# LSTM products moved behind the GRU's gates, routing to step 1, and a third bank for the expert products, in a one-core kernel of two recurrences, attention and a mixture of experts

## The chip, the cores and the metric

One core of one Trainium2 chip. The metric is the device time of one execution in microseconds (us). Median, lowest and highest of the runs are given below. All times in the text are us unless they say ns.

## The reference, cut to what matters

A block over a batch of 16 sequences of 128 steps, width 128:

```python
h   = LSTM(x, h0)                       # 128 steps, one after the other
x1  = x + causal_attention(h)           # 16 heads of 64, low-rank keys and values (32)
g   = GRU(x1, h0)                       # 128 steps; after every 4th: h = tanh(h @ Wp + bp)
out = x1 + sum over the top 2 of 8 experts of w_e * (gelu(g @ w1_e + b1_e) @ w2_e + b2_e)

# one step of the GRU
z, r = sigmoid([x_t, h] @ Wz + bz), sigmoid([x_t, h] @ Wr + br)
h_cand = tanh([x_t, r * h] @ Wh + bh)
h = (1 - z) * h + z * h_cand
```

Causality lets everything run as one pipeline: attention for a block of 8 steps needs only LSTM states up to it, the GRU needs only `x1` up to its step, the experts need whole blocks of 128 tokens (8 steps by 16 sequences).

## The kernel before, in words

The program is one loop over k, written out by hand for each engine: `for k in range(STEPS)` stands in the TensorE (PE), ScalarE (ACT), VectorE (DVE), GpSimd (POOL) and SyncE (SP) blocks. At k the LSTM does its step t = k and the GRU its step g = k - 18. Everything else is put into the loop at fixed residues of k modulo 8. I call these *step 0* to *step 7*. Each engine works its queue strictly in order, so that the order in the source is the schedule, and semaphores (`wait_ge`, `then_inc`) tie the queues together.

TensorE, per k: `g_step` (the GRU's gate products), then `turn_probs` (transposes of the attention's probabilities, steps 4 to 7, bank `pC`), `values` (steps 5, 6, 7, 0, bank `pV`), `project` (step 1), `lat_q` (step 0: latents into `pY`, queries into `pC`), an `experts_down` of slot A (bank `pV`, steps 2, 3, 4), then `g_candidate`, `l_step` (the LSTM's 12 recurrent products), `expert_up` half 0, `g_fill` (step 1), `experts_down` of slot B (bank `pY`, steps 2 to 6), `g_propagate`, `l_fill` (step 7: the LSTM's input products of the next eight steps, 9 products), `expert_up` half 1, `route_x` (step 2) and `scores` (steps 2 to 5). `expert_up` stands in steps 6, 7, 0 and 1.

The GRU's chain through the engines in one k: `g_step` (PE), `gT` = tanh (ACT), `gRZ` (DVE), `g_candidate` (PE), `gC` = tanh (ACT), `gB`, `ghi`, `g`, `glo` (DVE), next `g_step`. The LSTM's: `l_step`, `lT` (ACT), `lP`, `oK`, `lT[4]` (DVE), `lC` (ACT), `hhi`, `hfull`, `hlo` (DVE). A value is kept as a sum of two f16 parts (hi and lo), hence the three products for each matrix.

Waits that matter below:

- `expert_up` of half h waits until ScalarE has read the half before it out of the bank (`gelu`); on ScalarE that read (`activate`, tile `hid`) of half 1 stands behind `gC` and behind `pt_copy` (tile `PThi`).
- `lat_q` writes the latents into columns 384 to 511 of `pY`; `lat_copy` (DVE, tile `latT`) reads them. An expert product that goes into `pY` in this step waits for it: `pe.wait_ge(lat_done, count(latents_at, k + 1))`.
- `q_rest` (DVE, tile `qh`) ends the queries; SP then spreads them with four transfers for each group of four sequences (`spread_queries`, tile `qbd`), and `scores` waits for these.
- `TO_EXP` and `TO_GELU` name the k at which ScalarE changes its function table, with an activation into `spare`.

## Time and profile before

| | us |
|---|---|
| median of 3 runs | 589.99 |
| lowest, highest | 588.25, 590.3 |
| the profiled execution | 591.56 |
| its span in the profile | 589.7 |
| TensorE busy | 525.5 (89%) |
| VectorE busy | 424.1 (72%) |
| ScalarE busy | 352.9 (60%) |

The engines' shares are averages over three stages: LSTM and attention alone (k below 18, to about 63 us), the filling pipeline (k = 18 to 49, to about 190 us), and the full pipeline after that (to about 491 us), followed by a tail without the LSTM. The full pipeline repeats every eight k, so that one such period stands for all. Its time starts at the first product of `g_step` of step 0.

### The profile page before, as it was taken

Reading aid. Unit: us, or ns where it says so; the run is one execution under the profiler, and the core shown is the slowest. Engines: PE = TensorE matmul, PEld = TensorE weight load, DVE = VectorE, ACT = ScalarE, POOL = GpSimd, SP = SyncE. Lnnn points to the kernel's source line nnn. Section 1 sums busy time; section 2 is a strip of 40 time slices with the busy share of each in tenths; the row PEclk is TensorE's granted clock in tenths of the full one; section 3 lists DMA queues with packets and bytes.
Section 4 is the critical chain, followed back from the end, with each engine's and each line's share of the span. In section 5 each row is a group of like instructions: output and inputs, shape, how many; then the busy total and the mean of one; then the engine's idle time right before and its main releaser. Section 6 shows DMA issues by size and latency. Waiting matters only on the chain.

```text
span 589.7 us, 20148 instructions
## 1 busy us (share of the span) xinstructions
PE 525.5 (89%) x7315; PEld 483.4 (82%) x7356; DVE 424.1 (72%) x2402; ACT 352.9 (60%) x1297; POOL 33.6 (6%) x85
## 2 busy tenths in 40 slices
PE   7967887889789898989999989898999998889998
PEld 3736675888679898989888989898989988879998
DVE  4447678767776887878787878787879788664432
ACT  2235345775256676757676767676676767565562
POOL 6000000000000000000000000000000000000000
PEclk9679659699759999999999999999999999999999
DMA  8810101010100101010101010101101010100000
GB/s 204 327 15 6 20 1 20 3 13 10 16 11 6 16 5 17 12 20 3 19 12 17 7 15 16 12 10 12 16 14 13 4 17 13 18 1 3 11 7 10
DMA packets 75118, 14.32 MB, mean 24 GB/s; under 512 B 71411, under 2 KB 74111, under 8 KB 74638
## 3 DMA queue, kind: packets, MB, share of 16 engines
q1 hardware_dynamic: 74566, 11.96, 11.2%
q8 instruction: 60, 0.98, 0.7%
q10 hardware_dynamic: 456, 1.08, 0.6%
q14 instruction: 36, 0.29, 0.2%
HBM read 7.78 MB, written 1.05 MB: 15 GB/s over the span
## 4 chain that ended last, share of the span: by engine, by line
PE 68%; DVE 17%; issue 6%; ACT 6%; DMA 1%; SPq 1%; POOL 0%; DVEq 0%; ACTq 0%; POOLq 0%
PE pH L488 16%; PE pG L488 12%; PE pV L488 12%; PE pY L488 9%; PE pL L488 8%; PE pC L578 5%; PE pS L488 5%; ACT hid L864 2%; PE pC L488 2%; DVE latNlo L976 2%; DVE acc L1073 1%; DVE gB L1137 1%; DVE ghi L1140 1%; DVE glo L1143 1%; ACT gC L879 1%
## 5 line engine op out<-in xcount | busy, mean ns | idle before, releaser
L864 ACT ACTIVATE hid<-pH,b 128x256 f32<-128x256 f32 (+1 forms) x320 | 116.3, 433 | 3.9 <-PE pH L488 3.9
L488 PE MATMUL pY<-w,hid 128*128 128x128 f32 x608 | 85.1, 284 | 0.0
L488 PE MATMUL pH<-ghi,w1hi 128*128 128x256 f16 (+1 forms) x320 | 76.7, 254 | 9.1 <-ACT hid L864 7.3
L488 PE MATMUL pH<-ghi,w1lo 128*128 128x256 f16 (+1 forms) x320 | 77.0, 255 | 0.0
L488 PE MATMUL pH<-glo,w1hi 128*128 128x256 f16 (+1 forms) x320 | 76.9, 255 | 0.0
L488 PEld LDWEIGHTS pY<-w,hid 128*128 128x128 f32 x608 | 74.6, 193 | 0.2
L871 ACT ACTIVATE gT<-pG 128x32 f32<-128x32 f32 x128 | 24.7, 193 | 70.5 <-PE pG L488 70.3
L488 PE MATMUL pV<-w,hid 128*128 128x128 f32 x416 | 58.2, 283 | 0.0
L1124 DVE SCALAR_TENSOR_TENSOR gRZ<-gT,g 128x32 f32<-128x32 f32 x128 | 24.5, 191 | 46.6 <-ACT gT L871 46.0
L1137 DVE TENSOR_TENSOR gB<-gRZ,gC 128x16 f32<-128x16 f32 x128 | 22.5, 175 | 46.9 <-ACT gC L879 44.5
L879 ACT ACTIVATE gC<-pG 128x16 f32<-128x16 f32 x128 | 23.5, 183 | 52.9 <-PE pG L488 52.8
L488 PE MATMUL pG<-gRZ,gW 128*128 128x16 f32 x256 | 46.3, 257 | 7.4 <-DVE gRZ L1124 7.3
L488 PEld LDWEIGHTS pG<-gRZ,gW 128*128 128x128 f32 x256 | 41.7, 204 | 12.6 <-DVE gRZ L1124 12.0
L578 PE MATMUL pC<-ident,P 128*128 128x128 f32 x256 | 46.2, 309 | 6.4 <-DVE PTlo L988 5.1
L488 PEld LDWEIGHTS pV<-w,hid 128*128 128x128 f32 x416 | 50.9, 193 | 0.2
L488 PEld LDWEIGHTS pL<-hhi,lWhi 128*128 128x128 f16 x512 | 43.3, 118 | 8.2 <-DVE hhi L1157 6.9
L853 ACT ACTIVATE PThi<-pC 128x512 f16<-128x512 f32 x64 | 38.1, 595 | 19.7 <-PE pC L578 19.4
L882 ACT ACTIVATE lT<-pL 128x64 f32<-128x64 f32 x128 | 28.6, 223 | 34.4 <-PE pL L488 22.0
L488 PEld LDWEIGHTS pH<-ghi,w1hi 128*128 128x128 f16 x320 | 32.9, 103 | 14.9 <-DVE glo L1143 11.1
L488 PE MATMUL pL<-hhi,lWhi 128*128 128x16 f16 x512 | 41.6, 171 | 3.5 <-DVE hhi L1157 3.5
L988 DVE SCALAR_TENSOR_TENSOR PTlo<-pC,PThi 128x512 f16<-128x512 f32 x64 | 43.8, 685 | 0.7 <-issue 0.5
L488 PE MATMUL pL<-hhi,lWlo 128*128 128x16 f16 x512 | 41.2, 170 | 0.0
(177 smaller groups left out, 1569.6 us busy)
## 6 DMA issues: line engine op xcount, KB each, us to landing
w<-in_w SPq DMA_DIRECT2D x2, 2048.0 KB, 13.1
qbd<-qh SPq DMA_DIRECT2D x256, 16.0 KB, 1.9
out<-acc SPq DMA_DIRECT2D x16, 64.0 KB, 1.5
xT<-in_xT ACTq DMA_DIRECT2D x1, 960.0 KB, 8.2
hid<-in_WqT SPq DMA_DIRECT2D x1, 512.0 KB, 5.6
hid<-in_Wout SPq DMA_DIRECT2D x1, 512.0 KB, 10.3
lWh<-in_lWh SPq DMA_DIRECT2D x1, 256.0 KB, 2.8
lWx<-in_lWx SPq DMA_DIRECT2D x1, 256.0 KB, 3.1
```

The source lines that it names most:

```text
L488: return nc.tensor.matmul(o, lhsT=lhsT, rhs=rhs, start=start, stop=stop, skip_group_check=True)
L578: last = nc.tensor.transpose(pC[:, 128 * j:128 * (j + 1)], P[:, n % 2, j, :], ident[:, :])
L853: A(PThi[:, n % 2, :, :].rearrange("p j q -> p (j q)"), pC[:, :], ACT.Copy, scale=SH).then_inc(pt_done, 1)
L864: A(hid[:, e % NHID, c, 0:W], pH[half][:, W * at:W * (at + 1)], ACT.Gelu, bias=b1[:, e, c:c + 1], scale=1.0 / SP).then_inc(gelu, 1)
L871: A(gT[:, :, :], pG[:, 0:2, g % GS, :], ACT.Tanh, scale=1.0 / SP).then_inc(g_tanh, 1)
L879: A(gC[:, :], pG[:, 2, g % GS, :], ACT.Tanh, scale=1.0 / SP).then_inc(g_c, 1)
L882: A(lT[:, 0:4, :], pL[:, :, t % GS, :], ACT.Tanh, scale=1.0 / SP).then_inc(l_tanh, 1)
L976: V.transpose(turned[rows, :, 0:LD], whole_t[rows, :, 32 * j:32 * j + 32]).then_inc(latn_done, 1)
L988: V.scalar_tensor_tensor(PTlo[:, n % 2, :, :].rearrange("p j q -> p (j q)"), pC[:, :], SH, PThi[:, n % 2, :, :].rearrange("p j q -> p (j q ...
L1073: V.scalar_tensor_tensor(acc[:, m % 3, tg, :], bank_of(slot)[:, D * at:D * (at + 1)], gates[:, m % 3, tg, e:e + 1], acc[:, m % 3, tg, :], ...
L1124: V.scalar_tensor_tensor(gRZ[:, :, :], gT[:, :, :], 1.0, g8[:, at:last + 1:last - at, :], ALU.add, ALU.mult).then_inc(g_rh, 1)
L1137: V.tensor_tensor(gB[:, :], gRZ[:, 1, :], gC[:, :], ALU.mult).then_inc(g_b, 1)
```

## The change

It reorders work on TensorE, ScalarE and VectorE; the arithmetic stays but for small things.

- TensorE: `l_step` runs right behind `g_step` in every k. `l_fill` of step 7 runs ahead of `g_candidate`. `route_x` moves from step 2 to step 1. The expert products `(38, "B")` and `(46, "B")` (step 6) become `(40, "B")` and `(48, "B")` (step 0). Slot A of steps 2 and 3 uses `pC` in place of `pV`.
- VectorE: the LSTM's cell update (`cell`) runs ahead of `maximum`, the final products (`hidden`) right behind `glo`. `pt_rest` moves ahead of `gB`. `lat_copy` and `q_rest` move from ahead of `gB` into `between`, behind `normalise` and `turn_values`. The four instructions of `q_rest` become one. `turn_latents` moves from steps 1 and 2 to steps 2 and 3. `route_copy` leaves VectorE.
- ScalarE: `lT` right behind `gT`; `setup` and the table change of `TO_EXP` (now one step later, step 3) behind it; `lC` ahead of `gC`; `route_copy` at the end.

```diff
 DOWNS_TWO = ((34, "A", 0, 0), (34, "B", 0, 1), (35, "A", 1, 0), (35, "B", 1, 1), (36, "A", 2, 0), (36, "B", 2, 1),
-             (37, "B", 3, 0), (38, "B", 3, 1), (42, "A", 4, 0), (42, "B", 4, 1), (43, "A", 5, 0), (43, "B", 5, 1),
-             (44, "A", 6, 0), (44, "B", 6, 1), (45, "B", 7, 0), (46, "B", 7, 1))
-DOWNS_FIRST = ((34, "A"), (34, "B"), (35, "A"), (35, "B"), (36, "A"), (36, "B"), (37, "B"), (38, "B"))
+             (37, "B", 3, 0), (40, "B", 3, 1), (42, "A", 4, 0), (42, "B", 4, 1), (43, "A", 5, 0), (43, "B", 5, 1),
+             (44, "A", 6, 0), (44, "B", 6, 1), (45, "B", 7, 0), (48, "B", 7, 1))
+DOWNS_FIRST = ((34, "A"), (34, "B"), (35, "A"), (35, "B"), (36, "A"), (36, "B"), (37, "B"), (40, "B"))
...
-    at = GS * i + (26 if i < NG - 1 else 25)
-    if i > 12:
-        return at, at + 1, at + 2, at + 3, at + 3
-    return at, at + 1, at + 2, at + 6, at + 8
+    at = GS * i + 25
+    return (at, at + 1, at + 2, at + 3, at + 3) if i > 12 else (at, at + 1, at + 3, at + 7, at + 9)
+
+
+def down_bank(k, slot):
+    return "Y" if slot == "B" else "C" if k % TB in (2, 3) and k < LAST else "V"
...
-TO_EXP = [TB + O_S] + [k + 1 for k, half in UPS if half == 0 and (k + 1, 0) not in UPS and k < T]
+TO_EXP = [TB + O_S] + [k + 2 for k, half in UPS if half == 0 and (k + 1, 0) not in UPS and k < T]
...
-            def turn_probs(n):
+            def turn_probs(n, k):
                 pe.wait_ge(exp_done, 4 * (n + 1))
-                pe.wait_ge(q_lo, HG * (n // NU + 1))
+                pe.wait_ge(q_lo, n // NU + 1)
                 if n:
                     pe.wait_ge(pt_split, n)
+                if downs_before(k, "C"):
+                    pe.wait_ge(acc_done, downs_before(k, "C"))
...
-                        if downs_before(k, slot):
-                            pe.wait_ge(acc_done, downs_before(k, slot))
-                        if slot == "A":
+                        bank = down_bank(k, slot)
+                        if downs_before(k, bank):
+                            pe.wait_ge(acc_done, downs_before(k, bank))
+                        if bank == "V":
                             pe.wait_ge(on_done, count(lambda j: unit_at(j, O_V), k))
                             copied(k)
+                        elif bank == "C":
+                            pe.wait_ge(q_lo, count(latents_at, k))
                         else:
                             pe.wait_ge(lat_done, count(latents_at, k + 1))
-                    Y = bank_of(slot)[:, D * at:D * (at + 1)]
+                    Y = bank_of(k, slot)[:, D * at:D * (at + 1)]
...
 
-                if t < LAG:
+                if t < T:
                     l_step(t)
                 if unit_at(k, O_T) is not None:
-                    turn_probs(unit_at(k, O_T))
+                    turn_probs(unit_at(k, O_T), k)
                 if unit_at(k, O_V) is not None:
                     values(unit_at(k, O_V), k)
...
+                if t % GS == GS - 1 and LAG <= t and t + 1 < T:
+                    l_fill((t + 1) // GS)
                 if 0 <= g < T:
                     g_candidate(g)
-                if LAG <= t < T:
-                    l_step(t)
 
...
+            def route_copy(n):
+                m, tg = visit_of(n)
+                act.wait_ge(r_mm, n + 1)
+                if n >= 2:
+                    act.wait_ge(r_ranked, n - 1)
+                A(lg[:, n % 2, :], pV[:, 256:256 + E], ACT.Copy, scale=0.5).then_inc(r_copy, 1)
+                if slots_used(m, tg):
+                    act.wait_ge(stored[2 * (m % 3) + tg], 16 * slots_used(m, tg))
+                A(acc[:, m % 3, tg, :], pV[:, 384:512], ACT.Copy).then_inc(r_copy, 1)
...
                 if 0 <= g < T:
                     act.wait_ge(g_rz, g + 1)
                     A(gT[:, :, :], pG[:, 0:2, g % GS, :], ACT.Tanh, scale=1.0 / SP).then_inc(g_tanh, 1)
+                if t < T:
+                    act.wait_ge(l_gates, t + 1)
+                    A(lT[:, 0:4, :], pL[:, :, t % GS, :], ACT.Tanh, scale=1.0 / SP).then_inc(l_tanh, 1)
+                if k >= LAG:
+                    setup(k)
+                if k in TO_EXP:
+                    A(spare[:, 1:2], still[:, 0:1], ACT.Exp)
                 for m, e, chunks in UPS.get((k - 1, 0), []):
                     activate(m, e, 0, chunks)
                 early = unit_at(k, O_T) is not None and k >= LAG and (k - 1, 0) not in UPS
                 if early:
                     pt_copy(unit_at(k, O_T))
+                if t < T:
+                    act.wait_ge(l_c, t + 1)
+                    A(lC[:, :], lT[:, 4, :], ACT.Tanh, scale=0.5).then_inc(l_tc, 1)
                 if 0 <= g < T:
                     act.wait_ge(g_cand, g + 1)
                     A(gC[:, :], pG[:, 2, g % GS, :], ACT.Tanh, scale=1.0 / SP).then_inc(g_c, 1)
-                if t < T:
-                    act.wait_ge(l_gates, t + 1)
-                    A(lT[:, 0:4, :], pL[:, :, t % GS, :], ACT.Tanh, scale=1.0 / SP).then_inc(l_tanh, 1)
-                if unit_at(k, O_T) is not None and not early and k >= LAG:
+                if unit_at(k, O_T) is not None and not early:
                     pt_copy(unit_at(k, O_T))
-                if unit_at(k - 1, O_S) is not None and k >= LAG:
+                if unit_at(k - 1, O_S) is not None:
                     exps(unit_at(k - 1, O_S))
                 for m, e, chunks in UPS.get((k - 1, 1), []):
                     activate(m, e, 1, chunks)
                 if 0 <= g < T - 1 and g % 4 == 3:
                     act.wait_ge(g_prop, g // 4 + 1)
                     A(gp, pG[:, 3, (g + 1) % GS, :], ACT.Tanh, scale=1.0 / SP).then_inc(g_p, 1)
-                if t < T:
-                    act.wait_ge(l_c, t + 1)
-                    A(lC[:, :], lT[:, 4, :], ACT.Tanh, scale=0.5).then_inc(l_tc, 1)
-                if unit_at(k, O_T) is not None and k < LAG:
-                    pt_copy(unit_at(k, O_T))
-                if unit_at(k - 1, O_S) is not None and k < LAG:
-                    exps(unit_at(k - 1, O_S))
-                setup(k)
+                if k < LAG:
+                    setup(k)
                 if k in TO_GELU:
                     A(spare[:, 0:1], still[:, 0:1], ACT.Gelu)
-                if k in TO_EXP:
-                    A(spare[:, 1:2], still[:, 0:1], ACT.Exp)
                 if latents_at(k) is not None:
                     q_copy(latents_at(k))
                 if k in FIRST:
                     n = FIRST[k]
-                    act.wait_ge(r_low, n + 1)
-                    A(th[:, n % 2, :], low[:, n % 2, :], ACT.Tanh, scale=0.5).then_inc(r_th, 1)
+                    act.wait_ge(route[n % 2], 10 * (n // 2) + 1)
+                    A(th[:, n % 2, :], lg[:, n % 2, :], ACT.Tanh, bias=lmax[:, n % 2, 0:1]).then_inc(r_th, 1)
+                if k in ROUTES:
+                    route_copy(ROUTES[k])
...
             def q_rest(p):
                 dve.wait_ge(q_hi, p + 1)
-                for g in range(HG):
-                    V.scalar_tensor_tensor(qh[:, p % 2, :, 1, g, :],
-                                           pC[:, TOK * g:TOK * (g + 1)].rearrange("p (s b) -> p b s", b=B), 1.0 / SP,
-                                           qh[:, p % 2, :, 0, g, :], ALU.mult, ALU.subtract).then_inc(q_lo, 1)
+                V.scalar_tensor_tensor(qh[:, p % 2, :, 1, :, :],
+                                       pC[:, :].rearrange("p (g s b) -> p b g s", g=HG, b=B), 1.0 / SP,
+                                       qh[:, p % 2, :, 0, :, :], ALU.mult, ALU.subtract).then_inc(q_lo, 1)
...
             def between(k):
-                if unit_at(k, O_T) is not None:
+                if unit_at(k, O_T) is not None and k < LAG:
                     pt_rest(unit_at(k, O_T))
                 if unit_at(k, O_V) is not None:
...
                 if (k, "A") in DOWN_AT:
                     combine(k, "A")
+                if latents_at(k) is not None:
+                    lat_copy(latents_at(k))
+                if latents_at(k - 1) is not None:
+                    q_rest(latents_at(k - 1))
                 if k in FIRST:
                     route_first(FIRST[k])
                 if k in SOFT:
                     route_soft(SOFT[k])
-                if k % TB == 1 and TB < k <= T + 1:
+                if k % TB == 2 and TB < k <= T + 2:
                     turn_latents(k // TB - 1, lathi, latNhi)
-                if k % TB == 2 and TB < k <= T + 2:
+                if k % TB == 3 and TB < k <= T + 3:
                     turn_latents(k // TB - 1, latlo, latNlo)
...
+            def cell(t):
+                dve.wait_ge(l_tanh, t + 1)
+                V.scalar_tensor_tensor(lP[:, :, :], lT[:, 0:2, :], 1.0, lT[:, 3:5, :], ALU.add, ALU.mult).then_inc(l_mul, 1)
+                V.tensor_scalar(oK[:, :], lT[:, 2, :], SH / 2, SH / 2, ALU.mult, ALU.add)
+                dve.wait_ge(l_mul, t + 1)
+                V.scalar_tensor_tensor(lT[:, 4, :], lP[:, 1, :], 0.5, lP[:, 0, :], ALU.mult, ALU.add).then_inc(l_c, 1)
+
+            def hidden(t):
+                dve.wait_ge(l_tc, t + 1)
+                V.tensor_tensor(hhi[:, t + 1, :], oK[:, :], lC[:, :], ALU.mult).then_inc(l_hi, 1)
+                V.tensor_tensor(hfull[:, :], oK[:, :], lC[:, :], ALU.mult).then_inc(l_h, 1)
+                dve.wait_ge(l_h, t + 1)
+                V.tensor_tensor(hlo[:, t + 1, :], hfull[:, :], hhi[:, t + 1, :], ALU.subtract).then_inc(l_lo, 1)
...
                     V.scalar_tensor_tensor(gA[:, :], gT[:, 1, :], -1.0, prev, ALU.add, ALU.mult).then_inc(g_a, 1)
+                if t < T and k >= LAG:
+                    cell(t)
+                if unit_at(k - 1, O_S) is not None:
+                    maximum(unit_at(k - 1, O_S))
+                if t < T and k < LAG:
+                    cell(t)
                 if (k - 1, "B") in DOWN_AT:
                     combine(k - 1, "B")
+                if period_at(k) is not None:
+                    add_x(period_at(k))
                 if k >= LAG:
-                    after_latents(k)
-                if unit_at(k - 1, O_S) is not None:
-                    maximum(unit_at(k - 1, O_S))
+                    setup_late(k)
+                if unit_at(k, O_T) is not None and k >= LAG:
+                    pt_rest(unit_at(k, O_T))
                 if k in PICK:
                     route_pick(PICK[k])
                 if 0 <= g < T:
...
                     dve.wait_ge(g_h, g + 1)
                     V.tensor_tensor(glo[:, g, :], g8[:, g, :], ghi[:, g, :], ALU.subtract).then_inc(g_lo, 1)
                 if t < T:
-                    dve.wait_ge(l_tanh, t + 1)
-                    V.scalar_tensor_tensor(lP[:, :, :], lT[:, 0:2, :], 1.0, lT[:, 3:5, :], ALU.add, ALU.mult).then_inc(l_mul, 1)
-                    V.tensor_scalar(oK[:, :], lT[:, 2, :], SH / 2, SH / 2, ALU.mult, ALU.add)
+                    hidden(t)
                 if unit_at(k, O_V) is not None:
                     invert(unit_at(k, O_V))
-                if t < T:
-                    dve.wait_ge(l_mul, t + 1)
-                    V.scalar_tensor_tensor(lT[:, 4, :], lP[:, 1, :], 0.5, lP[:, 0, :], ALU.mult, ALU.add).then_inc(l_c, 1)
-                if k >= LAG:
-                    between(k)
-                if t < T:
-                    dve.wait_ge(l_tc, t + 1)
-                    V.tensor_tensor(hhi[:, t + 1, :], oK[:, :], lC[:, :], ALU.mult).then_inc(l_hi, 1)
-                    V.tensor_tensor(hfull[:, :], oK[:, :], lC[:, :], ALU.mult).then_inc(l_h, 1)
-                    dve.wait_ge(l_h, t + 1)
-                    V.tensor_tensor(hlo[:, t + 1, :], hfull[:, :], hhi[:, t + 1, :], ALU.subtract).then_inc(l_lo, 1)
-                if k < LAG:
-                    after_latents(k)
-                    between(k)
+                between(k)
                 setup(k)
-                if k in ROUTES:
-                    route_copy(ROUTES[k])
```

## Rows read from the trace of the kernel before

**Rows 1.** Windows: us, busy PE, PEld, DVE, ACT, POOL, granted clock, DMA share, GB/s.

```profile
275.50:306.50 31.00, 28.75 (x439) 27.53 (x438) 25.46 (x148) 21.09 (x76) 1.52 (x4) 1.00 0.11 15
...
18.00:190.80 172.80, 143.38 (x1935) 123.76 (x1955) 120.17 (x688) 88.14 (x352) 6.86 (x18) 0.76 0.14 31
```

**Rows 2.** Timeline of PE, k = 72 to 79 (steps 0 to 7): start, us, instruction [idle before].

```profile
275.50 0.17 PE L488 MATMUL pG<-ghi,gWhi 128*128 128x16 f16 x1
...
276.79 0.35 PE L488 MATMUL pG<-gRZ,gW 128*128 128x16 f32 x2
276.99 0.17 PE L488 MATMUL pL<-hhi,lWhi 128*128 128x16 f16 x1
...
277.29 0.27 PE L488 MATMUL pH<-ghi,w1hi 128*128 128x256 f16 x1
...
278.56 0.27 PE L488 MATMUL pH<-ghi,w1hi 128*128 128x256 f16 x1 [0.46 <-ACT hid L864]
...
279.22 0.17 PE L488 MATMUL pG<-ghi,gWhi 128*128 128x16 f16 x1
...
286.95 0.36 PE L488 MATMUL pV<-gateW,g 128*128 128x8 f32 x2 [0.86 <-DVE acc L1073]
...
288.46 0.22 PE L488 MATMUL pV<-b2P,onesP 128*128 128x128 bf16 x1 [0.44 <-DVE acc L1022]
...
296.41 0.40 PE L488 MATMUL pG<-gRZ,gW 128*128 128x16 f32 x2 [0.25 <-DVE gRZ L1124]
...
296.95 0.22 PE L488 MATMUL pY<-b2P,onesP 128*128 128x128 bf16 x1
...
297.95 0.29 PE L488 MATMUL pG<-g,gWp 128*128 128x16 f32 x2
...
298.52 0.62 PE L488 MATMUL pG<-g,gW 128*128 128x16 f32 x4
...
304.95 1.05 PE L488 MATMUL pL<-xT,lWx 128*128 128x128 f32 x8
...
306.50 0.17 PE L488 MATMUL pG<-ghi,gWhi 128*128 128x16 f16 x1
```

**Rows 3.** Timeline of ScalarE in steps 0, 6 and 7 of the same period.

```profile
277.17 0.18 ACT L879 ACTIVATE gC<-pG 128x16 f32<-128x16 f32 x1 [0.41 <-PE pG L488]
...
301.67 1.28 ACT L901 ACT_TABLE_LOAD   x1
302.97 0.20 ACT L901 ACTIVATE spare<-still 128x1 f32<-128x1 bf16 x1
...
304.38 0.59 ACT L853 ACTIVATE PThi<-pC 128x512 f16<-128x512 f32 x1
304.86 0.84 ACT L864 ACTIVATE hid<-pH,b 128x256 f32<-128x256 f32 x2
```

**Rows 4.** Timeline of VectorE in steps 0 and 5 of the same period.

```profile
276.32 0.29 DVE L960 TENSOR_SCALAR latT<-pY 128x128 f32<-128x128 f32 x1
...
277.39 0.18 DVE L1137 TENSOR_TENSOR gB<-gRZ,gC 128x16 f32<-128x16 f32 x1
...
278.71 0.31 DVE L1005 STREAM_TRANSPOSE OT<-On 128x128 f32<-128x128 f32 x1
...
297.36 0.17 DVE L1141 SCALAR_TENSOR_TENSOR g<-gA,gB 128x16 f32<-128x16 f32 x1
...
297.99 0.69 DVE L988 SCALAR_TENSOR_TENSOR PTlo<-pC,PThi 128x512 f16<-128x512 f32 x1
```

**Rows 5.** Timeline of SP's queue, step 1.

```profile
280.88 1.24 SPq L413 DMA_DIRECT2D qbd<-qh  x2
```

**Rows 6.** Tile qbd, 279 to 300 us: issue to landing.

```profile
DMA to landing us min/median/max: 1.9/2.0/2.6
```

**Rows 7.** Timeline of PE in k = 127, a step 7 that has no l_fill.

```profile
493.73 0.27 PE L488 MATMUL pH<-ghi,w1hi 128*128 128x256 f16 x1 [0.95 <-ACT hid L864]
```

**Rows 8.** Timeline of PE in k = 17, where the GRU's first inputs are awaited.

```profile
59.76 0.38 PE L488 MATMUL pG<-ind,biasP 128*128 128x512 bf16 x1 [1.66 <-DVE x1T L1012]
```

More of the change, by code:

```diff
@@ L117, in gelus_of, with downs_before @@
     return max(n for (vm, ve, h), n in GELUS.items() if (vm, ve) == (m, e))
-def downs_before(k, slot):
-    return max([ORDER[d] + 1 for (at, sl), ds in DOWN_AT.items() if sl == slot and at < k for d in ds], default=0)
+def downs_before(k, bank):
+    return max([ORDER[d] + 1 for (at, slot), ds in DOWN_AT.items() if down_bank(at, slot) == bank and at < k for d in ds], default=0)
 def count(at, upto):
@@ L245, in build @@
         lmax = sb("lmax", [128, 2, 1])
-        low = sb("low", [128, 2, E])
         th = sb("th", [128, 2, E])
@@ L374, in seq, with bank_of @@
             return t[:, :].rearrange("p (t b) -> p t b", b=B)[:, TB * p:TB * (p + 1), :].rearrange("p t b -> p b t")
-        def bank_of(slot):
-            return pV if slot == "A" else pY
+        def bank_of(k, slot):
+            return {"Y": pY, "C": pC, "V": pV}[down_bank(k, slot)]
         def keys(p):
@@ L742, in _ @@
                     g_propagate(g)
-                if t % GS == GS - 1 and t + 1 < T:
+                if t % GS == GS - 1 and t < LAG:
                     l_fill((t + 1) // GS)
@@ L1030, in route_first @@
                 V.tensor_tensor(gt[:, h, :, :], lj, li, ALU.is_gt).then_inc(r_cmp, 1)
-                dve.wait_ge(route[h], at + 1)
-                V.tensor_scalar(low[:, h, :], lg[:, h, :], lmax[:, h, 0:1], None, ALU.subtract).then_inc(r_low, 1)
             def route_soft(n):
@@ L1107, in setup_late @@
                     V.scalar_tensor_tensor(w1lo[:, e, :], w1[:, e, :], SW, w1hi[:, e, :], ALU.mult, ALU.subtract).then_inc(set_w1, 1)
-            def after_latents(k):
-                setup_late(k)
-                if latents_at(k) is not None:
-                    lat_copy(latents_at(k))
-                if latents_at(k - 1) is not None:
-                    q_rest(latents_at(k - 1))
-                if period_at(k) is not None:
-                    add_x(period_at(k))
+            def cell(t):
[10 more added lines that the diff above has]
+                V.tensor_tensor(hlo[:, t + 1, :], hfull[:, :], hhi[:, t + 1, :], ALU.subtract).then_inc(l_lo, 1)
             for k in range(STEPS):
```

27 lines of the change are left out of this document (9 added, 18 removed).

## The prediction, made before the result was known

> **What bounds the kernel now.** I read the windows of the page first. In the full pipeline a period of eight steps takes 31.00, TensorE is busy for 28.75 of them at a granted clock of 1.00, VectorE for 25.46, ScalarE for 21.09 [rows 1]. So TensorE's queue bounds this stage, and a reorder can win at most 31.00 - 28.75 = 2.25 in a period. Before that, from 18 to 190.8 us, TensorE is busy for 143.38 of 172.80 at a granted clock of 0.76, between its levels of 1.2 and 2.4 GHz; 0.24 x 172.8 x 2 = 83 us of it ran at 1.2 GHz [rows 1].
>
> Then I went through the timeline of one period, k = 72 to 79, engine by engine, with the source beside it. Its idle time has few places: step 0 waits 0.46 for ScalarE to empty the expert bank, step 2's `route_x` waits 0.86 for VectorE's `acc`, step 3's product 0.44 for the routing copy, step 5's candidate 0.25 for `gRZ` [rows 2]. All else is back to back. What matters for the change is therefore which of these waits go and which new ones the new order makes; I walk each step with the durations of the old one.
>
> Lengths in TensorE's stream, start to next start [rows 2]: the LSTM's products 277.29 - 276.99 = 0.30; a candidate 276.99 - 276.79 = 0.20; half an `expert_up` 279.22 - 278.56 = 0.66; a slot of expert products 297.95 - 296.95 = 1.00; `l_fill` 1.05.
>
> **Step 0: the product moved here waits for the latents.** It goes into `pY`, and so waits for `lat_copy` of the same k, which now stands at the end of VectorE's step. The candidate starts 276.79 - 275.50 = 1.29 into the step [rows 2], 1.59 with the LSTM's products ahead of it. `gC` follows after 277.17 - 276.79 = 0.38 [rows 2, 3], `gB` 0.22 later [rows 3, 4], the transpose `OT` 278.71 - 277.39 = 1.32 after `gB` (three LSTM instructions leave this stretch, three others enter it), takes 0.31, and `latT` takes 0.29 [rows 4]. Sum: 1.59 + 0.38 + 0.22 + 1.32 + 0.31 + 0.29 = 4.11. TensorE is there at 1.59 + 0.20 + 0.66 = 2.45: a stall of 1.7, with the other half of `expert_up` queued behind it. The step takes 4.11 + 0.05 for the semaphore + 1.00 + 0.66 = 5.82 against 279.22 - 275.50 = 3.72 [rows 2]: **+2.1**. The bounds: 1.1 is the stall less the old wait, 1.0 the moved product, which step 6 no longer has. If the stall were nothing, it would be +0.5.
>
> **Steps 6 and 7.** Now 306.50 - 298.52 = 7.98 together [rows 2]. The product leaves: -1.0. `l_fill` goes ahead of step 7's candidate, where TensorE had work enough, and leaves the place where it hid ScalarE's `gC`, `PThi` (0.59) and the two `hid` (0.84) [rows 3]. The row of that case exists: in k = 127 no `l_fill` follows, and the half waits 0.95 [rows 7]. There the LSTM's products (0.30) and `lT` were in the way on either side, which cancels: +0.95. Third, the table change at the end of step 6 (301.67 to 302.95 [rows 3]) ends as TensorE's longer step ends; with the step 1.0 shorter `gT` and `lT` of step 7 come late and `l_fill` waits for `lT`. I take +0.5, from 0 to 0.9. Together **+0.45**.
>
> ScalarE's other table change moves from the end of step 2 into step 3 ahead of `lC` and `gC`. Step 3 has two slots of products (2.0) around its candidate, which hide 1.28 + 0.20; that is nothing, and without the cover it would cost up to 0.7. The load ends at 302.95 and the next activation begins at 302.97 [rows 3], no more than 0.02 later. The Trainium skill (ScalarE: Activation LUTs, "What ACT_TABLE_LOAD costs") gives a drain of 1.38 besides the load; by it both changes would hold ScalarE 1.4 longer, and a period would be about 1 longer still. The row disagrees.
>
> **Steps 1 and 2.** `route_x` (about 0.36) changes its step, no change. In step 1 it waits for no combine: -0.86 [rows 2]. But `q_rest` now stands behind `hlo`. Step 1's candidate comes at about 0.15 + 0.30 + 1.0 (`project`) = 1.45, `gB` at 2.05, the six instructions to `hlo` take about 0.95, `q_rest` as one instruction of 512 columns about 0.69 (as `PTlo` [rows 4]): it ends at 3.7. SP issues a transfer each 1.24 / 2 = 0.62 [rows 5], so that the fourth goes at 5.55, and lands 2.0 later [rows 6]: 7.55. Step 2's `scores` are reached after 4.2 (step 1, an estimate) + 0.36 + 0.30 + 1.00 + 0.20 + 1.00 = 7.1. So +0.5, from 0 to 1.1 (a landing of 2.6 is seen too). Together **-0.35**.
>
> **Steps 3, 4, 5.** Step 3's wait of 0.44 goes, as the routing copy is off VectorE and long done; its product now waits for that of step 2 in the same `pC`, which VectorE combines behind `hidden` and the gates; the stall of step 2 covers it: **-0.4** (0 if not). Step 4's transposes go into `pC` too, and wait for the combine of step 3's product, at the end of VectorE's step 3: 0 to 0.6, I take **+0.4**. In step 5 the 0.25 goes. But `pt_rest` (0.69) and the cell (0.3) are now ahead of `gB`, and `g_propagate` needs `g`: now it ends at 297.53 and the product starts at 297.95 [rows 2, 4], a slack of 0.42. 0.69 + 0.30 - 0.42 = 0.57, plus the 0.1 by which the step is shorter up to there: +0.65, and only `scores` stands behind it. Together **+0.4** (bounds -0.25 and +0.9).
>
> Sum of a period: 2.1 + 0.45 - 0.35 - 0.4 + 0.4 + 0.4 = **+2.6**. The full pipeline has 300 / 31.0 = 9.7 periods: +25.
>
> **The rest.** In k = 17 the GRU's first inputs are awaited for 1.66 [rows 8]; `add_x` moves ahead of `hidden` and `q_rest`: -1. In k = 18 to 49: step 0 of k = 40 +1.1; k = 31 +0.95; k = 34 -0.9; `g` of four steps 5 (21, 29, 37, 45) 4 x 0.4; `l_fill` of k = 23 and 39, behind whose candidate no expert work stands, 2 x 0.8; the splits of `w1` on ScalarE (as long as `PThi`, 0.59) now ahead of `gC`, seven times some 0.3 = 2. That is +6, from 0 to 12. Without an LSTM (k above 127) only waits go: -1.
>
> Total: 25 + 6 - 1 - 1 = +29. The profiled execution took 591.56: 591.56 + 29 = 620.6. It lies 1.57 above the median of the runs, so that I forecast **619**. With the low bound of every term a period costs 2.1 - 0.05 - 0.86 - 0.44 - 0.25 = +0.5, with the high ones 2.1 + 0.85 + 0.24 + 0.6 + 0.9 = +4.7 (and the filling stage +12): 597 to 646. All terms don't fall to one side; the forecast's own range is 600 to 642.
>
> **The rivals.**
>
> 1. *Only the two walked stalls stand* (step 0, step 7), the late `g`, `pC` and the transfers are all covered, since each stall lets VectorE catch up. 2.1 + 0.95 - 1.0 - 0.86 - 0.44 - 0.25 = +0.5 in a period, +5, and +2 for the filling stage: 597. For it: VectorE has 5.5 idle in a period [rows 1]. Against: the late ones follow from the order in a queue. 14%.
> 2. *Faster: the waits go and none comes.* It would need `lat_copy` to end before TensorE asks, at 2.45 rather than 4.11, and step 7's half to find its bank empty. Then each period saves 0.46 + 0.86 + 0.44 + 0.25 = 2.0, 20 in all, and the start 1: 569. It decides at a stall of step 0 below about 0.8, a step 7 without one granted. The Trainium skill (Perfetto Trace Analysis, "Matmuls") asks for just what `pC` brings: independent groups rotate through banks, so that the emptying of one overlaps the products of the next. Here the third bank belongs to other work as well, and no row of before shows it free in step 4. 12%.
> 3. *The clock falls.* The filling stage had 1.2 GHz stretches with TensorE idle in 29 of 173 us [rows 1]. The full pipeline, at 1.00 so far, gets more and longer idle places, 33.6 - 28.75 = 4.85 in a period. At a granted clock of 0.86 the 28.75 of work grow by 4.7: another 45, 665. 8%.
> 4. *No change*: gains and stalls cancel, 590. 4%.
>
> **Numbers.** The forecast has 62%. 597 to 642 holds it and rival 1 and leaves out rivals 2, 3 and 4. 0.5% (3 us) is about what a measurement of this kernel tells from no change. Slower: 62 + 14 + 8 = 84%; same 4%; faster 12%.
>
> **What would show it.** In the profile after: in each step 0 from k = 56 on a product into `pY` that waits about 1.7 for VectorE's `latT`; in each step 7 a half of `expert_up` that waits about 1 for `hid`; in step 5 `g_propagate` waiting for `g`; in step 2 `scores` waiting for the `qbd` transfers; `route_x` without a wait; a period of 33.6. I am wrong if step 0's candidate comes much before 1.6 into the step, or if a period stays at 31 or below; or if the clock of the filling stage moves by much, since its 83 us at 1.2 GHz are worth up to 41.

## The result, and the profile after

| | before | after |
|---|---|---|
| median of the runs, us | 590.0 (588.25 to 590.3) | 636.33 (632.52 to 637.0) |
| span of the profiled execution, us | 589.7 | 634.5 |
| ratio of the times | | 1.0779, 95% interval 1.0731 to 1.0826 |

The kernel became slower by 46 us, on the side of the forecast, which was 619, and in the upper part of the range (597 to 642). The page of the kernel after, its head and the granted clock in 40 slices of the span:

```profile
span 634.5 us, 20164 instructions
...
PE 546.0 (86%) x7356; PEld 493.1 (78%) x7356; DVE 424.3 (67%) x2306; ACT 354.8 (56%) x1329; POOL 31.8 (5%) x85
...
PEclk9569556896559999999999999999989999999999
```

The windows view of the kernel after: the period k = 72 to 79, the stretch 18.00 to 190.80 of [rows 1], and four stages, cut at the start of ScalarE's `lT` of k = 18, 50 and 127 (columns as in [rows 1]):

```profile
292.33:326.48 34.15, 29.73 (x440) 27.66 (x438) 25.32 (x143) 20.89 (x78) 1.36 (x4) 1.00 0.09 12
18.00:190.80 172.80, 143.50 (x1833) 121.98 (x1832) 112.77 (x613) 83.39 (x338) 5.63 (x16) 0.69 0.13 30
...
18.00:61.28 43.28, 36.27 (x453) 26.96 (x453) 22.28 (x118) 16.10 (x65) 1.54 (x4) 0.73 0.27 89
61.28:201.01 139.73, 116.44 (x1516) 103.55 (x1515) 97.99 (x541) 73.12 (x295) 4.83 (x14) 0.69 0.08 10
201.01:534.04 333.03, 288.37 (x4213) 268.84 (x4213) 246.78 (x1369) 204.55 (x752) 12.89 (x38) 0.99 0.09 12
534.04:634.50 100.46, 90.15 (x1082) 85.71 (x1080) 48.18 (x240) 56.56 (x207) 2.64 (x8) 1.00 0.05 8
```

The same cuts in the kernel before fall at 64.88, 191.88 and 492.14: a filling stage of 127.0 (granted clock 0.77), a full one of 300.3, a tail of 97.6. So the 44.8 us by which the span grew are: -3.6 up to k = 18, +12.7 while the pipeline fills, +32.7 with all of it running, +2.9 behind the LSTM. The change itself moves `lT`: it stood 1.2 to 1.4 behind `gT` and now stands 0.3 to 0.1 behind it. Cut at `gT` instead, the four parts are -2.7, +12.9, +32.7 and +1.8. TensorE's busy time in the full period rose by 1.0, though the work is the same; the timeline will show why.

One period does not quite stand for all. From k = 55 on the periods of the kernel before grow from 30.9 to 31.5, and those of the kernel after from 34.1 to 35.1 (36.7 in the last one, with a fall of the clock, see the last section).

Now the same eight steps as [rows 2], in TensorE's timeline of the kernel after:

```profile
292.33 0.17 PE L488 MATMUL pG<-ghi,gWhi 128*128 128x16 f16 x1
...
293.12 0.18 PE L488 MATMUL pV<-latNhi,PThi 128*128 128x33 f16 x1 [0.20 <-issue]
...
294.26 0.35 PE L488 MATMUL pG<-gRZ,gW 128*128 128x16 f32 x2
294.46 0.27 PE L488 MATMUL pH<-ghi,w1hi 128*128 128x256 f16 x1
...
297.01 0.22 PE L488 MATMUL pY<-b2P,onesP 128*128 128x128 bf16 x1 [1.74 <-DVE latT L976]
...
306.31 0.18 PE L488 MATMUL pH<-cmask,ident 128*128 128x32 bf16 x1 [0.36 <-issue]
...
308.38 0.40 PE L488 MATMUL pG<-gRZ,gW 128*128 128x16 f32 x2
309.44 0.22 PE L488 MATMUL pY<-b2P,onesP 128*128 128x128 bf16 x1 [0.67 <-issue]
...
316.40 0.22 PE L488 MATMUL pY<-b2P,onesP 128*128 128x128 bf16 x1 [0.45 <-issue]
...
317.40 0.33 PE L488 MATMUL pG<-g,gWp 128*128 128x16 f32 x2
...
318.00 0.62 PE L488 MATMUL pG<-g,gW 128*128 128x16 f32 x4
...
321.18 0.18 PE L488 MATMUL pG<-ghi,gWhi 128*128 128x16 f16 x1
321.22 0.17 PE L488 MATMUL pG<-ghi,gWlo 128*128 128x16 f16 x1
321.25 0.17 PE L488 MATMUL pG<-ghi,gWhi 128*128 128x16 f16 x1
321.27 0.17 PE L488 MATMUL pG<-ghi,gWlo 128*128 128x16 f16 x1
321.47 0.21 PE L488 MATMUL pG<-glo,gWhi 128*128 128x16 f16 x2
...
321.85 0.26 PE L488 MATMUL pL<-hlo,lWhi 128*128 128x16 f16 x4
...
322.84 0.38 PE L488 MATMUL pL<-ind,biasP 128*128 128x512 bf16 x1
...
325.83 0.27 PE L488 MATMUL pH<-ghi,w1hi 128*128 128x256 f16 x1 [0.92 <-ACT hid L879]
```

Read from the top: step 0 starts at 292.33, and its product into `pY` begins only at 297.01, 1.74 behind the half of `expert_up`. Step 3's product into `pY` waits 0.67, step 5's 0.45, step 7's half 0.92. In step 7 the products of `glo` begin 0.20 after those of `ghi`, where the latter follow each other by 0.03. They wait for a piece of VectorE's step, and since a matmul of 16 columns counts as busy for 0.17, this wait appears as busy time and not as idle time. The long waits lose as much. The last product of `expert_up` in step 0 starts at 295.00 and the next could have followed 0.11 later; it starts at 297.01. So TensorE stood still for 1.90, of which the view shows 1.74 as idle. That 0.16 in each wait is a good part of the extra 1.0.

VectorE in the same kernel, the piece of step 0 that the product waits for, and the piece of step 3:

```profile
294.86 0.17 DVE L1158 TENSOR_TENSOR gB<-gRZ,gC 128x16 f32<-128x16 f32 x1 [0.54 <-ACT gC L904]
...
296.38 0.31 DVE L1020 STREAM_TRANSPOSE OT<-On 128x128 f32<-128x128 f32 x1
296.61 0.25 DVE L976 TENSOR_SCALAR latT<-pY 128x128 f32<-128x128 f32 x1
...
307.39 0.70 DVE L991 STREAM_TRANSPOSE latNhi<-lathi 32x512 f16<-32x512 f16 x1
308.13 0.19 DVE L1137 SCALAR_TENSOR_TENSOR gRZ<-gT,g 128x32 f32<-128x32 f32 x1
...
308.64 0.45 DVE L997 TENSOR_REDUCE mx<-pH 128x4 f32<-128x288 f32 x1
309.00 0.34 DVE L1077 SCALAR_TENSOR_TENSOR acc<-pY,gates,acc 128x128 f32<-128x128 f32 x1
```

In step 3 `acc`, which empties `pY` of step 2's product, stands behind the cell and the maximum and ends at 309.34; the product starts at 309.44. So, by the trace, this stall comes from VectorE's new order and the late `turn_latents` (307.39), and not from the third bank. No run here undoes these two.

### The profile page after: what moved, and what is told of

It reads as the page before. It is cut to its first block, busy times and chain, and to the rows that moved or that the text cites. A ratio compares the mean times of both kernels' runs of the same rounds, so it can differ in the third digit from the quotient of the medians.

```text
span 634.5 us, 20164 instructions
## 1 busy us (share of the span) xinstructions
PE 546.0 (86%) x7356; PEld 493.1 (78%) x7356; DVE 424.3 (67%) x2306; ACT 354.8 (56%) x1329; POOL 31.8 (5%) x85
## 4 chain that ended last, share of the span: by engine, by line
PE 78%; issue 8%; DVE 7%; ACT 6%; SPq 1%; DMA 0%; DVEq 0%; ACTq 0%
PE pH L488 17%; PE pY L488 15%; PE pG L488 12%; PE pL L488 10%; PE pV L488 7%; PE pC L488 6%; PE pC L580 6%; PE pS L488 5%; ACT hid L879 2%; DVE PTlo L1003 1%; ACT PThi L868 1%; SPq L413 1%; DVE ghi L1161 1%; ACT gC L904 1%; DVE gB L1158 1%
## 5 line engine op out<-in xcount | busy, mean ns | idle before, releaser
L488 PE MATMUL pH<-ghi,w1hi 128*128 128x256 f16 (+1 forms) x320 | 77.0, 255 | 14.9 <-ACT hid L879 12.6
L488 PEld LDWEIGHTS pH<-ghi,w1hi 128*128 128x128 f16 x320 | 36.0, 112 | 21.2 <-issue 17.8
L488 PEld LDWEIGHTS pG<-gRZ,gW 128*128 128x128 f32 x256 | 43.1, 210 | 5.1 <-DVE gRZ L1137 4.0
L488 PE MATMUL pY<-b2P,onesP 128*128 128x128 bf16 x76 | 16.5, 217 | 32.7 <-DVE latT L976 19.4
L488 PEld LDWEIGHTS pL<-hhi,lWhi 128*128 128x128 f16 x512 | 35.3, 103 | 7.6 <-DVE hhi L1126 6.3
L488 PEld LDWEIGHTS pY<-b2P,onesP 128*128 128x128 bf16 x76 | 8.7, 115 | 37.2 <-issue 37.0
```

The source lines that it names most:

```text
L488: return nc.tensor.matmul(o, lhsT=lhsT, rhs=rhs, start=start, stop=stop, skip_group_check=True)
```

## The experiments

The tables of this section give medians, ratios against runs of the kernel before on the same chip with their intervals, the stages cut as above, and the period k = 72 to 79 from `gT` to `gT`. The runs were taken in three lots, each with runs of the kernel before beside it; its median was 590.3, 592.5 and 591.3 in them. Small differences between lots are therefore taken from the ratios, as shares of 590 us. Stages and periods come from one profiled execution of each kernel.

| run | median | ratio, 95% interval | filling / full / tail | k = 72 to 79 |
|---|---|---|---|---|
| before | 590.0 | 1 | 127.0 / 300.3 / 97.6 | 31.00 |
| after | 636.33 | 1.0779, 1.0731 to 1.0826 | 139.7 / 333.0 / 100.5 | 34.15 |
| latents early | 611.44 | 1.0354, 1.0322 to 1.0385 | 133.1 / 315.2 / 99.0 | 32.51 |
| `l_fill` back | 624.29 | 1.0569, 1.0535 to 1.0603 | 134.6 / 327.2 / 100.5 | 33.36 |
| product back | 608.32 | 1.0313, 1.0293 to 1.0334 | 134.0 / 314.5 / 97.9 | 32.29 |
| `pt_rest` back | 640.06 | 1.0846, 1.0809 to 1.0882 | 138.0 / 336.4 / 99.9 | 34.53 |
| latents and `l_fill` | 602.67 | 1.0193, 1.0146 to 1.0240 | 127.9 / 311.1 / 99.1 | 33.14 (*) |
| all three | 594.63 | 1.0053, 1.0025 to 1.0080 | 126.4 / 304.2 / 97.9 | 31.29 |
| latents, `l_fill` and `l_step` back | 777.36 | 1.3140, 1.3095 to 1.3186 | 175.7 / 439.6 / 99.4 | 45.31 |
| before, product moved | 599.86 | 1.0129, 1.0089 to 1.0169 | 125.5 / 305.9 / 101.5 | 31.48 |
| that, latents late | 614.61 | 1.0394, 1.0359 to 1.0429 | 127.4 / 318.4 / 104.6 | 32.85 |
| before, bank and routing | 585.08 | 0.9891, 0.9865 to 0.9918 | 126.3 / 296.4 / 96.6 | 30.88 |
| that, product moved | 592.69 | 1.0010, 0.9981 to 1.0040 | 124.3 / 300.6 / 100.1 | 31.37 |
| bank, routing, two small ones | 585.09 | 0.9888, 0.9863 to 0.9914 | 127.2 / 295.8 / 96.5 | 30.60 |

(*) with a fall of the granted clock in k = 75 and 76, see the last section.

**From the kernel after: single parts undone.** First the latents' copy and `q_rest` ahead of `gB` again, for k from 18 on.

```diff
                     combine(k - 1, "B")
+                if latents_at(k) is not None and k >= LAG:
+                    lat_copy(latents_at(k))
+                if latents_at(k - 1) is not None and k >= LAG:
+                    q_rest(latents_at(k - 1))
                 if period_at(k) is not None:
...
-                if latents_at(k) is not None:
+                if latents_at(k) is not None and k < LAG:
```

> The changed kernel with lat_copy and q_rest ahead of add_x and gB again (from k = 18 on), nothing else. Theory (the read of the latents at the end of VectorE's step is what holds the moved product): the wait of 1.7 in step 0 goes in 11 periods, the scores' wait of about 0.35 in step 2 too, 2.1 to 2.2 in a period: 636 becomes about 611, the period 34.1 becomes 32.0. Rival (the LSTM's products right behind g_step expose hhi and hlo, and the time goes there whatever else is done): the stall moves on to the next wait, the period stays above 33.3 and the time above 628. Second rival (the longer filling stage and its half clock are the loss): the gain is below 10.

Measured 611.44: 25 less than after. The chain of effects is plain in the waits of TensorE, after and then in this run (what waited, for what: total us, times, the longest):

```profile
PE pY L488 <- DVE latT L976: 19.4, 11, 2.4
...
PE pH L488 <- ACT hid L879: 12.6, 15, 1.1
```

```profile
PE pY L488 <- issue: 14.1, 24, 0.9
PE pH L488 <- ACT hid L879: 12.6, 15, 1.2
```

The wait for `latT` is gone, that for `hid` is what it was. The wait itself is 19.4 of the 25: 1.74 in each of the nine steps 0 from k = 56 to 120, 2.4 at k = 40 and 1.4 at k = 128. The time was met closely, but not by the parts that I had named. The period fell by 1.6 to 32.51 and not to 32.0; the full stage gave 17.8, the filling stage 6.6 and the tail 1.4.

Second, `l_fill` back behind step 7's products.

```diff
-                if t % GS == GS - 1 and LAG <= t and t + 1 < T:
-                    l_fill((t + 1) // GS)
...
-                if t % GS == GS - 1 and t < LAG:
+                if t % GS == GS - 1 and t + 1 < T:
                     l_fill((t + 1) // GS)
```

> The changed kernel with l_fill behind the slot B products again for every k, as before. Theory: step 7's half of expert_up no longer waits 0.9 for its bank, in 10 periods: -9, about 627; the period 33.2. Rival (l_fill only changes places with another wait, since the candidate comes 1.05 earlier but ScalarE's queue is the bound): within 3 of the changed kernel, 633 to 639.

Measured 624.29, 12 less. TensorE's waits for `hid` go from 12.6 us in 15 to 2.2 in 4. The period falls by 0.79 to 33.36. Of the 10.6 by which the profiled span fell, only 5.8 lie in the full stage, and 5.1 in the filling stage.

Third, the expert products back in step 6, with all else as after.

```diff
-             (37, "B", 3, 0), (40, "B", 3, 1), ...
+             (37, "B", 3, 0), (38, "B", 3, 1), ...
```

> The changed kernel with the two slot B products in step 6 again (38 and 46), the latents still read late. Theory: no product waits for the latents; step 0 falls by the stall of 1.9 and by the product of 1.0, waits again 0.4 to 0.5 for its bank, and step 6 grows by less than 1.0, because VectorE and not TensorE sets it now: -1.5 to -2.0 in a period, about 618. Rival (the latents are not the cause, step 0 is long because the candidate is late): above 630.

Measured 608.32, 28 less, 10 more than expected. With no product into `pY` in step 0, nothing asks for the latents early, so that this takes the stall away too. The period fell by 1.86, which is what I expected, and the full stage by 18.5. The 10 more are the filling stage (5.7) and the tail (2.6), for which I had entered nothing.

Fourth, `pt_rest` behind the gates again.

```diff
-                if unit_at(k, O_T) is not None and k >= LAG:
-                    pt_rest(unit_at(k, O_T))
...
-                if unit_at(k, O_T) is not None and k < LAG:
+                if unit_at(k, O_T) is not None:
                     pt_rest(unit_at(k, O_T))
```

> The changed kernel with pt_rest in between (behind hidden) again. By the prediction pt_rest ahead of gB delays g and g_propagate in step 5 and the next g_step; the trace shows no wait for g there but small ones at hhi and hlo in steps 6 and 7. Theory (pt_rest ahead of gB puts hhi behind it and so the LSTM's products late): -0.3 to -0.6 in a period, 630 to 633. Rival (VectorE is full in steps 4 to 6 and the order of its work is of no matter): 634 to 638.

Measured 640.06: not faster, rather slower by 4, though the two intervals overlap. The new place of `pt_rest` costs nothing as a whole, and so my term for a late `g` in step 5 finds no support. The next transposes wait for the end of `pt_rest`; with it back at the old place, the waits view has this row, where the kernel after waits once, for 0.5:

```profile
PE pC L580 <- DVE PTlo L1003: 9.4, 18, 0.6
```

**Do the parts add up?** The latents and `l_fill` together:

> The changed kernel with both of the last two edits: latents read early and l_fill back. If the two waits are independent, the gains add: 636 - 25 - 12 = 599. If one covers the other, it stays near 611 - 5 = 606. What is then left over 590 is the loss of the rest of the order: the LSTM's products ahead, VectorE's new order, and the filling stage.

Measured 602.67: 33.7 less than after, where the two alone gave 25 and 12. They nearly add up (34.6 by the ratios). With the product back as well:

> The changed kernel with latents early, l_fill back and the products in step 6 again. What stays of the change: the LSTM's products behind the gates with ScalarE's and VectorE's order for it, the third bank, the routing at step 1 on ScalarE, the late table change. Theory (the moved product costs 0.5 to 0.9 in a period, since step 6 has time for it): 602.7 - 7 = 596. Rival (with the new order TensorE sets step 6): 601 or more.

Measured 594.63: the third edit gives 8 more, not 28. Of its 28, then, 20 were the stall that the early latents also remove. What the change contains beyond these three costs 0.53% of 590, or 3.1 (interval 1.5 to 4.7); 594.6 - 590.0 would say 4.6, but the kernel before had 591.3 beside these runs. The filling stage is back at 126.4, and its clock with it (the windows of this run, filling and full stage):

```profile
60.20:186.60 126.40, 105.27 (x1502) 95.30 (x1515) 97.67 (x541) 72.39 (x294) 5.11 (x14) 0.80 0.09 11
186.60:490.80 304.20, 282.86 (x4199) 268.75 (x4216) 247.40 (x1369) 203.56 (x751) 12.88 (x38) 1.00 0.10 13
```

I looked for this rest in the LSTM's place on TensorE: latents early and `l_fill` back, and the LSTM's products behind the candidate again, on TensorE alone.

```diff
-                if t < T:
+                if t < LAG:
                     l_step(t)
...
                     g_candidate(g)
+                if LAG <= t < T:
+                    l_step(t)
```

> The kernel of the run before (latents early, l_fill back) and besides l_step behind g_candidate again on TensorE, with ScalarE and VectorE as in the changed kernel. Theory (the LSTM's products directly behind g_step wait for hhi and hlo, some 0.3 in each of steps 6, 7, 0): these waits go, but lT now comes late on ScalarE, ahead of its other work, and the cell ahead of gB waits for it: no better, 598 to 606. Rival (the place of l_step on TensorE is the loss): at or below 592.

Measured 777.36, far outside what either theory said. Its waits, the first ones of ScalarE and VectorE that stand in the recurrences:

```profile
ACT lT L889 <- PE pL L488: 193.0, 127, 4.8
DVE lP L1119 <- ACT lT L889: 163.3, 125, 3.1
ACT gT L886 <- PE pG L488: 127.6, 87, 3.7
```

ScalarE now has `lT` right behind `gT`, ahead of `gC`, and VectorE the cell ahead of `gB`. With `l_step` behind the candidate, whose `gRZ` comes from `gT`, the GRU's next value waits for the LSTM's products in each of the 110 k in which both run: two recurrences that ran side by side run one after the other. In k = 72 to 79 the period is 45.31. A part of the 777 is the clock: TensorE ran at 1.2 GHz for about 115 us of the full stage (0.87 granted over 439.6), where the kernel before had none, and for 109 us of the filling stage (0.69 over 175.7), where that one had 58. So TensorE's order, `lT` behind `gT` and the cell ahead of `gB` are one edit, and this run says nothing of the rest.

**From the kernel before: parts of the change alone.** The product moved to step 0, with the latents' copy early as in the kernel before.

> The kernel before with one part of the change alone: the slot B products of step 6 go to step 0 (40 and 48); there lat_copy is early. Theory: the place itself is good. The wait of 0.46 in step 0 is filled, step 6 loses 1.0 of TensorE's work, of which VectorE and the table change take back most: -0.2 to -0.4 in a period, 586 to 589. Rival (moving the product costs in itself): 593 or more.

Measured 599.86: 1.3% or 7.6 us more (599.9 - 590.0 is 9.9, but the kernel before had 592.5 beside it), where a small gain or nothing was expected. I had taken the moved product for a mere exchange, 1.0 less in step 6 and 1.0 more in step 0. But step 6 of k = 78 is as long as before (`gT` to `gT` 3.90, before 3.91): ScalarE's exponentials and the table change set its length, and the product lay in their shadow. In step 0, `gT` to `gT`, it adds 0.38, and in step 1 another 0.09: 0.48 in a period, about 5 in the full stage. The profiled execution also has a lower clock in k = 59, 135 and 136, where that of the kernel before has none, so that not all of its time is the product's. TensorE's waits show where it now stands idle in its place: for `gRZ` 13.7 us in 29 waits, against 7.3 in 18 before.

```profile
PE pG L488 <- DVE gRZ L1124: 13.7, 29, 2.2
PE pV L488 <- DVE acc L1073: 10.6, 12, 1.1
```

Then the same with `lat_copy` at the end of VectorE's step, as the change has it:

```diff
                 if k >= LAG:
                     between(k)
+                    if latents_at(k) is not None:
+                        lat_copy(latents_at(k))
```

> The kernel before with the products moved to step 0, as in the run with that part alone (599.9), and besides lat_copy behind between, at the end of VectorE's step. It shows the stall of step 0 by itself, with VectorE, ScalarE and TensorE otherwise in the old order. Theory (the late read alone makes the stall, whatever the order around it): TensorE waits about 1.4 for the latents in each of 11 steps 0, nothing gives it back: 612 to 617. Rival (the stall needs the new order, with hidden ahead of it): below 606.

Measured 614.61, 14.8 above the run with the product alone (15.6 by the ratios). The wait that the kernel after has appears out of these two edits:

```profile
PE pY L488 <- DVE latT L960: 14.3, 11, 1.9
```

14.3 us of waits and about 15 us of time: here the stall costs just its length, and it needs neither the LSTM's new place nor VectorE's new order.

Now the routing at step 1 and the third bank, with nothing else:

```diff
+def down_bank(k, slot):
+    return "Y" if slot == "B" else "C" if k % TB in (2, 3) and k < LAST else "V"
...
-    at = GS * i + (26 if i < NG - 1 else 25)
+    at = GS * i + 25
```

> The kernel before with two parts of the change alone: the third bank pC in steps 2 and 3, and the routing at step 1. Against the run that had the moved products too (592.7) the products are back in step 6, where they cost nothing. Theory: the waits of 0.86 and 0.44 go and about 0.6 of them comes back as the wait for the combine in pC: 583 to 586. Rival (VectorE is the bound from step 2 to 6): 589 to 592.

Measured 585.08, 1.1% faster than before. The row `PE pV <- DVE acc L1073` with its 10.6 us, above, is no longer among this run's waits; these are the first two:

```profile
PE pG L490 <- DVE gRZ L1131: 12.7, 19, 2.4
PE pH L490 <- ACT hid L871: 7.4, 14, 1.0
```

The wait for the routing copy (`acc L1022`, 5.0 us in 13 waits before) is down to 0.5 in one. So 15 us of waits go, of which 6.4 arrive as time (1.1% of 590). The wait for `gRZ` alone grows from 7.3 to 12.7, and `pC` brings 4.0 of its own. The timeline of TensorE in this run shows three such places in k = 72 to 79:

```profile
284.59 0.22 PE L490 MATMUL pC<-b2P,onesP 128*128 128x128 bf16 x1 [0.27 <-issue]
286.36 0.40 PE L490 MATMUL pG<-gRZ,gW 128*128 128x16 f32 x2 [0.61 <-DVE gRZ L1131]
292.62 0.63 PE L582 MATMUL pC<-ident,P 128*128 128x128 f32 x4 [0.24 <-DVE acc L1080]
```

A product waits 0.27 for the bank `pC`, the candidate of k = 75 waits 0.61 for `gRZ`, and the transposes wait 0.24 for the combine in `pC`. The Trainium skill (Perfetto Trace Analysis, "Matmuls") wants independent groups in several banks. The gain of 1.1% agrees with it, as far as bank and routing, which no run here parts, can be taken together.

With the product moved on top:

> The kernel before with three parts of the change: the products moved to step 0, the third bank pC in steps 2 and 3, and the routing at step 1 (the copy still on VectorE at the end of its step). Theory: the waits of 0.86 and 0.44 in steps 2 and 3 go too, -1 in a period against the run with the moved product alone: 576 to 582. Rival (TensorE's waits only change places, VectorE is the bound in steps 2 to 6, and the product of step 3 waits for the combine of step 2 in pC): 586 to 590.

Measured 592.69: the 7 us or so come back, as without the bank. I had expected that the bank makes the move free. It does not: from `gT` to `gT` step 6 stays at 3.91 (3.90 with bank and routing alone), while step 0 takes 4.09 for 3.72.

Last, a version that might beat both: bank and routing, `q_rest` as one instruction, `add_x` ahead of the LSTM's final products while the pipeline fills. The "run before" of this expectation is bank and routing alone (585.08).

> The kernel of the run before, and besides q_rest as one instruction and, for k below 18, add_x ahead of hidden. In the changed kernel the GRU's start came 3.6 us earlier, which I put down to these two. Theory: 3 less than the run before, 580 to 583. Rival (the earlier start came from ScalarE's order or is taken back by the clock in the filling stage): the same as the run before.

Measured 585.09, the same as without the two small edits. k = 18 starts 1.0 sooner than in the kernel before and 0.5 sooner than with bank and routing alone (`gT` at 62.7, 63.7 and 63.2). That is no sure gain: five kernels here have the same code up to k = 18, and there it starts at 62.3 to 65.7.

## Why the prediction was right, and what it had wrong

The sign and the main mechanism stand: the walked stalls of step 0 and step 7 are there and go when their cause is undone. The sum came out 17 short (619 against 636), and some terms were right only together. By terms:

- *Step 0, predicted +2.1.* Measured 6.33 for 3.72, +2.6; the stall 1.74 for 1.7. Of the missing 0.5, `values` makes 0.33: it follows the LSTM's products only at 293.12 (0.20 of it shown as idle), behind VectorE's late `On` of step 7 (`normalise`, which empties `pV`), so that the candidate comes at 1.93 into the step and not at 1.59. Neighbouring steps hand their delay on; I had let each step start clean. The late latents are borne out by themselves: added to the moved product, they lengthen a period by 1.37, and I had 1.1.
- *Steps 6 and 7, predicted +0.45.* Measured 8.48 for 7.98, +0.50. In TensorE's order step 6 takes 3.18 for 4.08, and step 7 takes 5.30 for 3.90. That is near my three terms, -1.0, +0.95 and +0.5, and the half does wait 0.92 for the 0.95 of [rows 7]. The cause of the +0.5 is another one. The load ends at 322.36, `lT` ends at 322.78, and `l_fill` starts at 322.84, right behind `values`: it was not held. Late are `glo` and `hlo` from VectorE, which come behind `pt_rest`, and with them the transposes (322.07). In the kernel before the table change does set the time: the run that moves the product alone gets nothing back in step 6, so that there the table change had to be entered as +1.0.
- *Steps 1 and 2, predicted -0.35.* Measured -0.46. `route_x` has no wait, and step 2's `scores` wait 0.36 for 0.5. `q_rest` ends 3.64 into step 1, predicted 3.7, and `scores` start at 7.65, predicted 7.55.
- *Step 3, predicted -0.4.* Measured +0.56. Here the argument failed. I looked only at who uses `pC`. The wait is in `pY`, for a combine that VectorE reaches late. The miss of 0.96 in a period, times 9.7, is 9 us.
- *Steps 4 and 5, predicted +0.4 each.* Measured -0.01 and -0.05. Both waits that I had entered are absent. `g_propagate` (317.40) doesn't wait for `g`, since its product ahead is itself late by 0.45, for a combine again. The transposes start at 311.31, when the combine that empties `pC` has been over since 310.68: the stall of step 3 lies between. So steps 3 to 5 came out at +0.50 together for +0.4, and that is luck: one wait was there that I had left out, and two were not.
- *A period*: 34.15 - 31.00 = +3.15 for +2.6; the full stage +32.7 for +25, since the difference grows to 3.7 in the later periods.
- *The filling stage, predicted +6.* Measured +12.7. Its granted clock went from 0.77 over 127.0 us to 0.69 over 139.7: 58 and 87 us at 1.2 GHz, 29 more. With all three edits undone it is 0.80 over 126.4, 51 us. A stretch at 1.2 GHz lasts up to twice as long, so that 29 us are worth up to 14. But two things say that the waits make most of the 12.7 and the clock the smaller part. With `pt_rest` back the filling stage has only 61 us at 1.2 GHz, near the 58 of before, and still takes 138.0:

```profile
61.31:199.35 138.04, 110.83 (x1516) 98.22 (x1515) 96.30 (x541) 72.74 (x294) 4.84 (x14) 0.78 0.08 10
```

  And of the four runs of the kernel after, the one with a granted clock of 0.932 took 632.5, the three with 0.909 to 0.914 took 636.3 to 637.0: some 27 us less at 1.2 GHz for 4 us, an estimate from their clocks and spans. No run holds the order fixed and changes the clock. Rival 3 does not explain the result: in the full stage, where I had put it, there are 3.4 us at 1.2 GHz (last section).
- *The start, predicted -1.* Measured -3.6, of which 0.9 is only `lT` that moved; k = 18 starts 2.7 sooner by `gT`. It starts at 59.5 to 61.9 in the eight kernels that have the changed code up to there, and at 62.3 to 65.7 in the five that have the old code, so that the gain is about 3. Which part of the order gives it stays open: with `add_x` early and `q_rest` as one instruction it starts at 62.7, within the old spread.
- *The tail, predicted -1.* Measured +2.9. The expert products of k = 128 and 136 moved as well, and at k = 128 there is a stall of 1.35 for the latents. With the latents early the tail is 99.0, with the product back 97.9.

One of the recorded sums is off. With the low bound of every term, +0.5 in a period and nothing in the filling stage, the time would be 593 and not 597; the result lies at the other end of the range.

The table load: the rows of ScalarE in step 6 and 7 of the kernel after,

```profile
321.08 1.28 ACT L917 ACT_TABLE_LOAD   x1
322.38 0.20 ACT L917 ACTIVATE spare<-still 128x1 f32<-128x1 bf16 x1
...
322.56 0.22 ACT L889 ACTIVATE lT<-pL 128x64 f32<-128x64 f32 x1
```

again have 0.02 between the load's end and the next activation. By the Trainium skill (ScalarE: Activation LUTs, "What ACT_TABLE_LOAD costs") a drain of 1.38 would stand there; the trace shows none.

**What stays open**: the last 3.1 us of the version with three edits undone. The bank and the routing alone give 6.4 of gain, so that the LSTM's place with the new order on ScalarE and VectorE costs about 9.5, if the parts add up. In k = 72 to 79 of that run TensorE waits 0.34 in `pC` in step 2, 0.68 in `pY` in step 3 and 0.43 in `pY` in step 5. From `gT` to `gT` its step 3 takes 3.86, and 3.19 with bank and routing alone; the late combine would be about 7 us in 10 periods. That is argued from the traces; a version with the combine ahead of the cell was not run.

## What to carry to other kernels

Before moving work into another slot, look which engine sets the length of the slot that it leaves: work in a shadow frees nothing (here 7 to 8 us lost for "1.0 less here, 1.0 more there"). For each bank that moved work writes, and not only for the one that the change names, list everything that reads the bank and where this stands in its engine's queue. And an engine that takes results in a fixed sequence ties the others to it: here two recurrences interleave on three engines, and with the order changed on two of them and not on TensorE, 603 us became 777. Last, compare the parts of a sum with the parts of the result, and not only the totals: twice here (steps 3 to 5, and the latents early) the total was close and the parts were not.
